# Two attention blocks and a feed-forward block on one TensorE: three score banks in the full passes, one ring of product banks, another order of the products, and an earlier load of the second batch

## The reference, cut to what matters

```python
# 16 batches, 256 tokens, width 256, 16 heads; ctx: the same for layer 0 and for cross-attention
x = LN(softmax(mask(q0(x) @ k0(ctx).T / 8)) @ v0(ctx) @ Wo + bo + x)         # heads of 64: stream A
x1 = LN(x  + attention(q(x),  k(x),    v(x), mask) @ o)                     # heads of 16: stream B
x2 = LN(x1 + attention(cq(x1), ck(ctx), cv(ctx)) @ co)                      # heads of 16: stream C
out = LN(x2 + relu(x2 @ lin1 + b1) @ lin2 + b2)                             # 256 -> 1024 -> 256
```

## Time and profile before

| | us |
|---|---|
| median of 3 runs | 1893.57 (1890.61 to 1894.02) |
| profiled execution | 1884.11 |
| its span, first to last instruction | 1882.4 |
| PE busy | 1739.3 (92%) |
| DVE busy | 1304.5 (69%) |
| ACT busy | 1197.7 (64%) |
| POOL busy | 986.1 (52%) |

### The profile page before, as it was taken

The page is one execution under the profiler, slowest core; times in us unless marked ns, Lnnn a source line. Parts: engine busy times, 40 slices in busy tenths (PEclk is TensorE's granted clock), DMA queues, the critical chain, the costliest instruction groups (busy, mean ns, idle before and its releaser), DMA issues.

```text
span 1882.4 us, 37642 instructions
## 1 busy us (share of the span) xinstructions
PE 1739.3 (92%) x11456; PEld 1298.9 (69%) x11456; DVE 1304.5 (69%) x5194; ACT 1197.7 (64%) x3985; POOL 986.1 (52%) x1030
## 2 busy tenths in 40 slices
PE   7799999999999999999999999999999999998887
PEld 5666677676766767677676776767677676776565
DVE  4365777686867768676777768778676877757863
ACT  3264676666666676766666676666766666666752
POOL 3143555646555464655546464555646555454842
PEclk9999999999999999999999999999999999999989
DMA  7421416575665857566575756757576675703110
GB/s 156 116 91 64 141 64 218 159 248 167 207 214 165 264 168 237 168 201 227 164 259 162 222 174 197 243 161 260 147 229 196 189 244 164 225 29 124 68 57 12
DMA packets 223174, 319.97 MB, mean 170 GB/s; under 512 B 31488, under 2 KB 192000, under 8 KB 214784
## 3 DMA queue, kind: packets, MB, share of 16 engines
q1 hardware_dynamic: 219856, 317.55, 54.1%
q10 hardware_dynamic: 3120, 0.01, 0.1%
HBM read 166.49 MB, written 151.00 MB: 169 GB/s over the span
## 4 chain that ended last, share of the span: by engine, by line
PE 53%; DVE 17%; DMA 13%; SPq 6%; ACT 5%; issue 5%; POOL 0%; DVEq 0%; POOLq 0%; ACTq 0%
PE ps_gd L657 22%; PE ps_ga L657 9%; PE ps_s L777 7%; PE ps_t L794 7%; PE ps_av L817 7%; DMA p_kept<-blocks 6%; DVE prob L1076 5%; DMA prob_b<-p_kept 4%; ACT prob L899 3%; SPq L570 3%; SPq L553 3%; DVE blocks L1099 2%; DMA k_parts_B<-k_hl 2%; DVE res_ln L1052 2%; DVE stats_ln L1037 2%
## 5 line engine op out<-in xcount | busy, mean ns | idle before, releaser
L1201 POOL TENSOR_TENSOR prob<-prob,recip 128x512 f32<-128x512 f32 x768 | 786.3, 1045 | 729.4 <-DVE recip L1087 725.0
L899 ACT ACTIVATE prob<-prob,ext 128x256 f32<-128x256 f32 x1536 | 757.7, 499 | 45.0 <-DVE ext L1076 42.8
L909 ACT ACTIVATE prob_t<-ps_t 128x512 f32<-128x512 f32 x384 | 227.0, 595 | 388.4 <-PE ps_t L794 387.2
L794 PE MATMUL ps_t<-ident,prob 128*128 128x128 f32 x1920 | 305.7, 284 | 5.3 <-DVE prob_b L1108 5.1
L899 ACT ACTIVATION_READ_ACCUMULATOR prob<-prob,ext 128x1 f32 x1536 | 295.0, 192 | 0.0
L794 PEld LDWEIGHTS ps_t<-ident,prob 128*128 128x128 f32 x1920 | 219.4, 142 | 89.7 <-issue 44.0
L1076 DVE CUSTOM_DVE_ANT_0 prob<-ps_s,mask_a 128x256 f32<-128x256 f32 x512 | 186.7, 421 | 117.0 <-PE ps_s L777 113.3
L1076 DVE CUSTOM_DVE_ANT_0 prob<-ps_s,mask_b 128x256 f32<-128x256 f32 x512 | 186.7, 420 | 85.3 <-PE ps_s L777 84.4
L1076 DVE CUSTOM_DVE_ANT_0 prob<-ps_s,zero 128x256 f32<-128x256 f32 x512 | 185.9, 419 | 69.7 <-PE ps_s L777 69.7
L1099 DVE STREAM_TRANSPOSE blocks<-prob 128x512 f32<-128x512 f32 x288 | 185.3, 681 | 7.7 <-DMA p_kept<-blocks 7.3
L777 PE MATMUL ps_s<-k_ctx,q 64*128 64x256 f32 x1024 | 145.5, 402 | 12.2 <-DVE ext L1076 7.6
(11 more groups left out here) (98 smaller groups left out, 2779.4 us busy)
## 6 DMA issues: line engine op xcount, KB each, us to landing
p_kept<-blocks SPq DMA_DIRECT2D x576, 128.0 KB, 2.4
prob_b<-p_kept SPq DMA_DIRECT2D x144, 512.0 KB, 3.4
k_parts_C<-k_hl SPq DMA_DIRECT2D x64, 256.0 KB, 4.5
k_parts_B<-k_hl SPq DMA_DIRECT2D x64, 256.0 KB, 2.8
k_B<-k_parts_B SPq DMA_DIRECT2D x16, 1024.0 KB, 6.3
q_parts_B<-q_hl SPq DMA_DIRECT2D x64, 256.0 KB, 6.4
q_B<-q_parts_B SPq DMA_DIRECT2D x16, 1024.0 KB, 5.4
q_parts_C<-k_hl SPq DMA_DIRECT2D x64, 256.0 KB, 6.6
```

The costliest lines, as they stand in the source:

```text
L794: last = nc.tensor.transpose(two(ps_t[e])[:, kt, qt * P:(qt + 1) * P], src[:, e, qt, kt * P:(kt + 1) * P], ident[:, :])
L899: last = nc.scalar.activation(tile, tile, ACT.Exp, bias=ext[:, slot, e, t:t + 1], scale=-1.0, accum_out=sums[:, slot, e, t:t + 1])
L909: nc.scalar.activation(prob_t[:, e], two(ps_t[e]), ACT.Copy).then_inc(copied_second, 1)
L1201: nc.gpsimd.tensor_tensor(rows, rows, recip[:, slot, e].unsqueeze(2) .to_broadcast([P, TT, TOK]), ALU.mult).then_inc(normed[s], 1)
```

## The change

- **Score banks.** In full passes the scores turn in three banks, ps_s0, ps_s1 and ps_av: head e of the pair at place number p goes to bank (2p + e) mod 3. The scores of the next pair wait for the first head of this one only. In the other passes all is as before.
- **Weighing.** In full passes it writes into ps_t1, the bank of the second turn. That turn (T1) now waits until the weighing before it has been taken out.
- **Product banks.** All jobs turn in one ring of three banks, ps_g0 to ps_g2, and each waits for the third before it.
- **Order.** The table of steps is another one (below).
- **Second batch.** In pass 1 the residual from x_tok (POOL) and the load of the next input stand at the head of the pass, instead of in A7; k's second product goes from pass 0 to pass 1's A0. `load` also waits for the transposes of x.

```diff
     after = {
-        ("A", 0): late + [job("ks"), dma("save k", "B"), ln("ln1")],
-        ("A", 1): [dma("k", "B"), job("qs"), dma("save q", "B")],
-        ("A", 2): [dma("q", "B"), job("x2T"), job("v", 0)],
-        ("A", 3): [job("qc"), dma("save q", "C"), job("k", 2), job("q", 2)],
+        ("A", 0): late + [dma("save k", "B"), job("ks"), dma("save q", "B")],
+        ("A", 1): [dma("k", "B"), job("qs"), ln("ln1"), job("v", 0)],
+        ("A", 2): [job("x2T"), dma("q", "B"), job("q", 2), job("qc"), io("value_c")],
+        ("A", 3): [job("k", 2), dma("save q", "C"), job("v", 1)],
         ("A", 4): [dma("q", "C"), job("oc"), job("vs")],
-        ("A", 5): [io("value_c"), ln("ln2"), job("v", 1)],
+        ("A", 5): [ln("ln2")],
         ("B", 0): [job("x3T"), job("v", 2)],
-        ("B", 1): [job("hd"), job("h", 0), res("res3", 0)],
-        ("C", 0): [job("h", 1), res("res3", 1)],
-        ("C", 1): [job("q", 3), res("res2", 0)],
-        ("B", 2): [job("h", 2), res("res2", 1)],
-        ("B", 3): [job("k", 3), res("res1", 0)],
-        ("A", 6): [half("y"), res("res1", 1)],
-        ("A", 7): [job("y"), res("res0", 0)],
-        ("C", 2): [io("load"), job("v", 3), ln("ln3")],
-        ("C", 3): [io("store"), job("kc")],
-        ("B", 4): [job("vc")],
-        ("B", 5): [io("save_c"), job("xT")],
-        ("B", 6): [job("cT")] + [half("wo")] * closed,
+        ("B", 1): [res("res3", 0), res("res3", 1), job("h", 0)],
+        ("C", 0): [job("hd")],
+        ("C", 1): [job("h", 1), job("q", 3), res("res2", 0), res("res2", 1)],
+        ("B", 2): [],
+        ("B", 3): [res("res1", 0), job("k", 3), job("h", 2)],
+        ("A", 6): [half("y"), res("res1", 1), res("res0", 0)],
+        ("A", 7): [],
+        ("C", 2): [job("y")],
+        ("C", 3): [io("load"), job("kc")],
+        ("B", 4): [job("v", 3), io("save_c"), io("store"), job("vc")],
+        ("B", 5): [job("xT"), job("cT"), ln("ln3")],
+        ("B", 6): [half("wo")] * closed,
         ("B", 7): [job("wo")] * closed,
-        ("C", 4): [ln("ln0"), job("q", 0, "x")] * closed,
-        ("C", 5): [job("k", 0, "x")] * closed,
-        ("C", 6): [job("q", 1, "x")] * closed,
+        ("C", 4): [job("k", 0, "x")] * closed,
+        ("C", 5): [job("q", 0, "x")] * closed,
+        ("C", 6): [job("q", 1, "x"), ln("ln0")] * closed,
         ("C", 7): [job("k", 1, "x")] * closed,
     }
 
+    if present == {"x", "a"}:
+
+        after = {place: [x for x in jobs if x[1:3] not in (("res0", 0), ("load", 0))] for place, jobs in after.items()}
+        after["A", 0] = [job("k", 1)] + after["A", 0]
+        head += [res("res0", 0), io("load")]
+    if present == {"x"}:
+        first = first[:3]
...
-            return ps_gd[(body.base[1] + body.banks.index(("J",) + step[1:])) % 2]
+
+            return ps_g[(body.base[1] + body.banks.index(("J",) + step[1:])) % 3]
...
+        def score_bank(body, step, e):
+
+            if body.full:
+                return (ps_s + [ps_av])[(2 * body.place(step) + e) % 3]
+            return ps_s[e]
+
+        def weigh_bank(body):
+
+            return ps_t[1] if body.full else ps_av
...
-                past = body.earlier(step, 2 if step[1] in DVE_JOBS else 1, ring[step[1]])
+                past = body.earlier(step, 3, lambda s: s[0] == "J" and s[1] != "mask")
...
-                    pe.wait_ge(masked[s0], count(b0, HEADS, 2 * p0 + 2))
+
+                    same = body.full and (body.pairs.index(step) or body.before.full)
+                    pe.wait_ge(masked[s0], count(b0, HEADS, 2 * p0 + (1 if same else 2)))
...
+                if e == 1:
+                    last = [x for x in body.steps[:body.steps.index(step)] if x[0] == "W"]
+                    if last and body.full:
+                        pe.wait_ge(ctx_out[last[-1][1]], count(body.batch(last[-1]), QUADS, last[-1][2] + 1))
```

More of the change, by code:

```diff
@@ L320, in earlier @@
             return None
-        if self.present == set("xabcm"):
+        if self.full:
             assert past[i] == mine[i]
@@ L772, in scores @@
                     (_, s0, p0, _), b0 = past
-                    pe.wait_ge(masked[s0], count(b0, HEADS, 2 * p0 + 2))
+                    same = body.full and (body.pairs.index(step) or body.before.full)
+                    pe.wait_ge(masked[s0], count(b0, HEADS, 2 * p0 + (1 if same else 2)))
+                if body.full and not body.before.full and step == body.pairs[0]:
+                    _, s0, quad0, _ = weighing = [x for x in body.before.steps if x[0] == "W"][-1]
+                    pe.wait_ge(ctx_out[s0], count(body.before.batch(weighing), QUADS, quad0 + 1))
                 for t in range(TT):
@@ L791, in turn @@
                     pe.wait_ge(copied_second, 2 * (quad - 1) + e + 1)
+                if e == 1:
+                    last = [x for x in body.steps[:body.steps.index(step)] if x[0] == "W"]
+                    if last and body.full:
+                        pe.wait_ge(ctx_out[last[-1][1]], count(body.batch(last[-1]), QUADS, last[-1][2] + 1))
+                    elif not last and body.before and body.before.full:
+                        last = [x for x in body.before.steps if x[0] == "W"]
+                        pe.wait_ge(ctx_out[last[-1][1]], count(body.before.batch(last[-1]), QUADS, last[-1][2] + 1))
                 for kt in range(TT):
```

30 lines of the change are left out of this document (14 added, 16 removed).

## The result

The change makes the kernel faster: median 1828.95 us (1823.82 to 1833.80, four runs) against 1893.80 us of the kernel before on the same chip (1890.61 to 1896.29, four runs); the ratio is 0.966 (0.963 to 0.969). Predicted was 1847, with a range from 1826 to 1870. The profiled execution took 1833.8 us, with a span of 1832.1; it was the slowest of its four. Its span is 50.3 us less than that of the profiled execution before, where the medians differ by 64.9.

What follows compares the result with a forecast made beforehand. PE, busy 92% of the span, was taken as the bound. Per full pass 3.0 + 0.6 - 0.3 - 0.2 - 0.4 + 0.9 = 3.6 us; twelve give 43, with the ends 47: 1893.6 - 47 = 1847 us, range 1826 to 1870.

Steps and rivals of the forecast that it cites:

- half clock behind them: Full passes: four 3.4 us half-clock stretches behind PE's 2.08 us waits for extremes go; plus 0.6 us a pass.
- tight places B2 and A7, the turn that waits for the weighing: Full passes: places left without a product, and a turn waiting for the weighing's evacuation; 0.3 us a pass set aside.
- half wo: Its wait for ACT's evacuation of the last A context stays, 1.2 us instead of 1.0; minus 0.2 a pass.
- x3T: Transposes in B0 newly wait for ln2 from A5, which loses its covering product v1; minus 0.4 us a pass.
- The first wait: PE's scores, mainly at B4 and C6, wait for DVE's extremes behind ln3 and ln0; all 3.0 us a pass go.
- rival 5: Third score bank unused, the order alone acts; B2 and A7 wait 0.7 us each; 1864 us, chance 0.06.
- The third wait: A0 to B1: weighings wait for loaded-back probabilities, 1.1 us instead of 2.0 for both; plus 0.9 a pass.
- Rival 4: Changing banks chops PE's work, bringing a half-clock stretch in every pass; 1874 us, chance 0.04.
- The banks of the products: The ring of three brings nothing in full passes; at the ends four waits go, 4 us.
- The ends: Starting and closing passes: product-bank waits 4 us, early input 0.6, less about 1 for places without product; plus 3.6.
- The first and third: First: transfers land as now, 1864 us, chance 0.17. Third: v load in A2 makes SP's queue the bound, 1914, chance 0.08.
- The second: More goes than counted: both weighings find their data, x3T and half wo wait for nothing new; 1823 us, chance 0.09.

Runs made afterwards that it cites:

- both heads version: The changed kernel with three score banks, but scores wait for both heads of the pair before; 1838.72 us, ratio 0.974 to the kernel before.
- last version: The changed kernel with the load of v for C in A5 and the feed-forward's two weight loads behind the second batch's input; 1817.79 us, ratio 0.962.
- the shift, v load and weights together: The changed kernel with q, k and v products shifted (A1 loses one), v load in A5, feed-forward weights behind the second batch's input; 1824.35 us.
- q0 in B6: The changed kernel with the next batch's first q product moved from C5 to B6, ahead of half wo; 1831.96 us, ratio 0.964.
- the banks alone: The changed kernel with the kernel before's table of steps and the late input; 1870.69 us, ratio 0.990 to the kernel before.

## Why the prediction was right, and where it was not

**The sum.** For the profiled execution it gave 1837 us, and 1833.8 were measured; for the median it gave 1847, and 1829.0 were measured. The difference of 9.5 us that I carried from the one to the other is a step that failed: the profiled execution before lay 9.5 us below its median, the one after 4.9 above. With all the runs later taken of it, the kernel before lies between 1883.9 and 1904.3 us. The offset did not stay, and a part of it at least was no constant of the measurement.

Part of it has a likely cause on record. In the 30 later runs of the kernel before, the slower ones had the lower mean granted clock: the five at 0.986 or 0.987 took 1883.9 to 1890.0 us, the four at 0.980 or less 1897.5 to 1904.3, and the middle one of all had 0.983. The profiled execution had 0.987, as high as any. From 0.987 down to 0.983 is some 15 us more at half clock, which costs 7.5 us (my estimate: 0.004 of 1884 us, times two, halved). The changed kernel's four runs had 0.986 to 0.989. So the profile before probably showed too few of the half-clock stretches that the 2.08 us waits bring, and the term for them, 0.6 us a pass, was too small for a median run. No trace of a slower execution was taken, so it is not shown where their half clock lay.

**A full pass.** Predicted 107.2 us, measured 106.1. Term by term, a pass:

| term | predicted | measured |
|---|---|---|
| extremes (S:B4, S:C6, S:A6, S:B5) | +3.0 | +3.25 |
| half clock behind them | +0.6 | +0.46 |
| not named: the rest of the change in PE's busy time | 0 | +0.37 |
| tight places B2 and A7, the turn that waits for the weighing | -0.3 | 0 |
| half wo | -0.2 | -0.15 |
| x3T | -0.4 | -0.34 |
| W:A0 and W:A1 | +0.9 | +1.2 |
| not named: W:B3 waits for its load-back | 0 | -0.1 |
| sum | +3.6 | +4.7 |

The extremes are 3.0 by their row; the rest of the 3.25 is 0.2 at S:A6, for which the trace names no releaser, and gaps too small for a row. The half clock is four stretches less one, at 1.7 us each. PE's busy time fell by 0.8 a pass, and the 0.4 that is left has no cause on record; the ends of matmuls are modelled, and there are fewer waits.

- *The first wait* was read rightly: ln3 and ln0 stood between DVE and the next extremes, and their new places have cover. That the third bank carries the places without a product was also right: without the early release they cost 1.3 us a pass, where rival 5 had 0.7 each. The 0.3 us set aside was not needed in the eleven passes.
- *The turn that waits for the weighing* does not wait in the eleven passes, but the mechanism exists: 0.59 us as soon as C5 has no product, and 0.78 us once in the first full pass of the changed kernel, for ACT's evacuation of C's weighing. The prediction had named 0.5 us of this wait as a sign of being wrong.
- *The third wait* was laid out rightly: load-back issued at 32 to 33 (measured 31.9 to 33.8), landed at 38 to 39 (37.1 to 40.5), asked for at 38.2 (38.1). It was mis-sized by 0.3 us, since A0's weighing no longer waits, and only six passes of eleven wait at A1, 0.77 us a pass in place of 1.1 for both. The 1.1 was more than the layout itself gives: a landing at 38 to 39 with the ask at 38.2 is a wait of at most 0.8, and A0's load-back was laid out to land before its ask.
- *The half clock.* The clock was granted in full from 434.5 to 1649.6 us, as forecast but for one stretch, 431.1 to 434.5 in pass 5, behind the wait of 2.42 us for the load-back:

```profile
434.50:1649.60 1215.10, 1188.65 (x7940) 892.52 (x7939) 910.10 (x3684) 843.59 (x2834) 700.70 (x717) 1.00 0.64 203
```

  Rival 4 falls with this row: three score banks and three product banks turn at every step, and the granted clock never left 2.4 GHz in it. In the eleven passes of all fourteen profiles 18 stretches were at half clock, and each lies at one wait of PE of 2.0 to 3.5 us: for the extremes in the kernel before, for a load-back in the others. Seven of the eleven waits of 2.08 us had none. The rule of the Trainium skill (TensorE: Matmul & The Clock Gate, "A second HAM failure mode: psum-queue depth-cycling") is not borne out here; the page describes a kernel with bf16 matmuls of 512 columns, and these are f32 with 256 or 128.
- *The banks of the products*: "nothing comes of it there" is the reasoning that failed. I looked for bank waits in the trace of the old order, found none, and did not ask whether the new order makes one. It puts two of ACT's products side by side, and with the old banks they would have cost 1.0 us a pass. The sum came out all the same, because I had charged neither the wait nor the ring that holds it off. Had only the table been changed, a sum made like mine would have been some 11 us too good for this wait alone.

**The ends.** Predicted +3.6 us, measured -1.7 between the two profiled executions (1.0 ahead of the full passes, 0.7 behind). Much of that is scatter of the start: the both heads version has the same instructions up to the first full pass and reached it at 275.7 us instead of 282.0, with 6.8 us at half clock instead of 17.0 and a shorter stop in its first pass (last section). With that start the ends would have gained 4.6. So the profiles neither bear out nor refute the 3.6, and this slow start may be a part of the 14.6 us. The twelfth full pass, the first one, is a step apart: the sum gave it 3.6 like the others, and it gained 0.3. It has new waits of 0.83 us at its first scores, where the one use of the banks passes into the other, 0.78 at a second turn 12 us later, 0.61 at W:A1 and 0.67 at W:B3.
- The four waits for the one ACT bank are gone, with the size that I gave them: 0.93 twice ahead of x1T, 1.26 and 0.93 at h in the last pass. But the ends are chains in which PE waits every few microseconds, and what it no longer waits for in one place it waits for in the next: ks after x1T 0.43 instead of 0.22 and 0.14, C3's scores in pass 3 0.75, C7's in the last pass 0.75, oc 0.36. At the ends I had counted removed waits without asking what is late next.
- More of the ends ran at half clock in this execution: 17.0 us instead of 10.2 ahead of the full passes, 34.2 instead of 26.4 behind them, where PE is busy for 237.8 us instead of 235.8.
- The early input brought nothing, rightly forecast: landed at 67.4, 0.6 us behind the second weight. The wait was to be 9 to 10 us with an issue at 53, and was 6.4 with an issue at 54.6. PE did not come 4 us sooner, since it had stood still before, for something not in the sum (last section).

**The rivals.** The first and third (the transfers) fall with the landing at 38.5. The second (more goes than counted) is the one towards which the result leans: A1's weighing finds its data in five passes of eleven, and in ten of the last version, but x3T and half wo kept their waits in both. The fifth falls with the both heads version.

**What stays open.** Where the 14.6 us lie by which the medians differ more than the two profiles: the clock of the kernel before and the start of the changed one are the candidates above. Why the load-back of A2's quad takes 5.0 us in one pass and 7.3 in another, with the same bytes and nearly the same issue, was not settled, nor whether the load of v for C has a part in when it lands. Nor was a version tried in which turn and weighing keep banks of their own; all eight are in use.

## What to carry to other kernels

When a change comes with a new order and new buffers, lay the new order over the old buffers as well: the trace before only shows the waits of the old order, and a pair of neighbours that one engine empties is a new one. Where a product is taken away from one place to cover a wait in another, look up what it had covered: here each of three attempts gave back what it won, at a shared bank or at a transfer that lands when it lands. For a transfer at the start, count what stands ahead of it in the queue, not how early it is issued. And before a difference between a profile and the median goes into a sum, compare the granted clock of the profiled run with that of the others.

## What was not expected of the hardware

In the first pass of the changed kernel three engines stand still for microseconds with their inputs there. ACT evacuates k's third product 8.34 us after its last exponential, though PE had finished it at about 28; PE's scores wait for that, and SP's issue of one weight load takes 8 us at the same time (the one behind it takes 5.0, those at 53 us 0.5):

```profile
23.22 8.01 SPq L617 DMA_DIRECT2D w_cv<-L_xattn_cv_w  x1
...
33.95 0.84 ACT L913 ACTIVATE k_ctx<-ps_g,col_bk 128x256 f32<-128x256 f32 x2 [8.34 <-remote]
...
34.89 1.90 PE L796 MATMUL ps_s<-k_ctx,q 64*128 64x256 f32 x8 [4.83 <-ACT k_ctx L913]
```

The releaser is given as remote, that is, nothing in this kernel's dependences. DVE shows 4.10 us of the same kind, up to 30.59. The kernel before shows 1.39 us on DVE alone, at 31.4. All eleven other versions with the new order of the first pass show such a stop of ACT; it ends between 31.2 us (the shift, v load and weights together) and 35.3 (q0 in B6). So the 3.5 us that this order had gained by 29.5 were lost again before the second batch's input mattered. It coincides with the weight loads, but they are not enough: with the banks alone, which has the old order, the same issue takes 8.1 us, and no wait of ACT is given as remote. A candidate seemed to be in the page's list of queues, which names two that carry instructions:

```profile
q8 instruction: 96, 1.57, 0.4%
q14 instruction: 102, 0.84, 0.1%
```

If an engine's next instructions came through transfers that stand among the weights, it would look like this. The trace speaks against it: between 0.5 and 39.5 us of the changed kernel no packet of these two queues is on record, only 8196 of q1 and 3120 of q10; their first ones start at 39.8 and 40.1, after the stop. The cause stays open.
